# Second Mamba stage: C rows spread over partitions by DMA from DRAM, the leaky relu as a relu and one product more, sums in two banks, five chunks under way

## The reference, cut to what matters

```python
h = _mamba(_ln(src, n1_g, n1_b), ...)
src = src + _ln(h, mnorm_g, mnorm_b)
f = _ln(src, n2_g, n2_b) @ ffn_w1.T                     # 128 -> 512
f = jnp.where(f >= 0, f, 0.01 * f) @ ffn_w2.T           # leaky relu, 512 -> 128
src = src + f
src = src + (_ln(src, n3_g, n3_b) @ fe_w.T + fe_b)

# in _mamba, 16 states n for each of 128 features d:
x_c = silu(x_prev * conv_w[:, 0] + x_in * conv_w[:, 1] + conv_b)
dt, B, C = split(x_c @ x_proj_w.T, [64, 80])
delta = softplus(dt @ dt_proj_w.T + dt_proj_b)
h[d,n](t) = exp(delta[d] * A[n]) * h[d,n](t-1) + delta[d] * B[n] * x_c[d]
y[d] = sum over n of h[d,n] * C[n]
y = (y + x_c * Dp) * silu(z);  out = y @ out_proj_w.T
```

## Time and profile before

| | us |
|---|---|
| median of 3 runs | 3508.48 (3506.49 to 3509.16) |
| the profiled execution, its own time | 3504.51 |
| its span, first to last instruction | 3502.4 |
| first scan of MB | at 1870.30 |
| end of the last scan of MB | at 2315.7 |
| last weighting and add of M2's second pass | at 2539.16 |

### The profile page before, as it was taken

One profiled execution on the slowest core, in us unless ns is written; L12 is line 12 of the kernel. 1 busy time (PEld: TensorE's weight loads), 2 busy tenths in 40 slices (PEclk: granted clock), 3 DMA queues, 4 the chain that ended last, 5 costly groups with the idle time before them and its releaser, 6 DMA issues. The chain is left out here.

```text
span 3502.4 us, 45735 instructions
## 1 busy us (share of the span) xinstructions
PE 3090.4 (88%) x15266; PEld 1928.3 (55%) x15266; DVE 2466.9 (70%) x5491; ACT 2035.3 (58%) x3494; POOL 672.1 (19%) x547
## 2 busy tenths in 40 slices
PE   7998999998999996799887777778899998799998
PEld 5775334333777652256543333345477776577776
DVE  5557777773645877777666878776777777677776
ACT  4442767666445445444346766644387777277776
POOL 1020110100000000000003544430033333023332
PEclk9999999999999998889998999999999999799999
DMA  2000121110100320023330000013411110011011
GB/s 85 1 26 21 53 71 59 62 59 30 33 1 26 109 83 0 0 84 99 102 108 23 1 0 1 1 35 96 147 35 49 43 31 28 10 36 46 31 47 52
DMA packets 99186, 159.66 MB, mean 46 GB/s; under 512 B 16220, under 2 KB 28956, under 8 KB 98824
## 3 DMA queue, kind: packets, MB, share of 16 engines
q1 hardware_dynamic: 97368, 153.86, 14.1%
q10 hardware_dynamic: 1584, 2.88, 0.2%
HBM read 138.67 MB, written 17.99 MB: 45 GB/s over the span
## 5 line engine op out<-in xcount | busy, mean ns | idle before, releaser
L394 POOL TENSOR_TENSOR norm_rstd<-norm_rstd,minus_half 128x4 f32<-128x4 f32 x144 | 177.2, 1230 | 1530.6 <-DVE norm_rstd L385 1527.9
L2404 ACT ACTIVATE main_tiles_r<-banks,feature_cols 128x512 fp32r<-128x512 f32 x512 | 352.7, 689 | 186.5 <-PE banks L245 165.3
L2412 DVE TENSOR_TENSOR main_tiles_r<-main_tiles,main_tiles_r 128x512 fp32r<-128x512 f32 x512 | 382.9, 764 | 68.3 <-ACT main_tiles L2405 66.8
L243 PE MATMUL banks<-normed_pairs,moe_weights 128*128 128x512 f32 x800 | 407.8, 510 | 13.1 <-ACT main_tiles L2405 6.5
L955 DVE TENSOR_REDUCE gate_scratch<-banks 128x2 f32<-128x1024 f32 (+2 forms) x320 | 345.7, 1114 | 101.3 <-PE banks L234 51.5
L1113 ACT ACTIVATE main_tiles<-banks 128x512 f32<-128x512 f32 (+1 forms) x608 | 317.3, 578 | 154.9 <-PE banks L1099 56.4
L2405 ACT ACTIVATE main_tiles<-banks,feature_cols 128x512 f32<-128x512 f32 x512 | 349.9, 683 | 0.0
L2449 POOL TENSOR_TENSOR normed<-normed,main_tiles 128x512 f32<-128x512 f32 x128 | 217.7, 1700 | 532.0 <-DVE main_tiles L2438 532.0
L244 PE MATMUL banks<-normed_pairs,moe_weights 128*128 128x512 f32 x800 | 317.7, 397 | 0.0
L245 PE MATMUL banks<-normed_pairs,moe_weights 128*128 128x512 f32 x800 | 317.6, 397 | 0.0
L243 PE MATMUL banks<-main_tiles_r,moe_weights 128*128 128x512 f32 x640 | 267.4, 418 | 29.3 <-DVE main_tiles_r L2412 26.7
(11 more groups left out here) (355 smaller groups left out, 6851.9 us busy)
## 6 DMA issues: line engine op xcount, KB each, us to landing
main_tiles<-gates_d SPq DMA_DIRECT2D x400, 256.0 KB, 3.3
found_d<-main_tiles SPq DMA_DIRECT2D x32, 256.0 KB, 2.0
parts_d<-bf_parts SPq DMA_DIRECT2D x48, 128.0 KB, 1.8
q_stacks<-parts_d SPq DMA_DIRECT2D x192, 32.0 KB
k_stacks<-parts_d SPq DMA_DIRECT2D x192, 32.0 KB
weight_staging<-in_w SPq DMA_DIRECT2D x22, 256.0 KB, 3.8
attn_tiles<-in_w ACTq DMA_DIRECT2D x11, 256.0 KB, 7.6
x_res<-in_x_t SPq DMA_DIRECT2D x8, 256.0 KB, 9.2
```

The costliest lines, as they stand in the source:

```text
L243: eng.matmul(o, wh, hi, start=first, stop=False)
L394: eng.tensor_tensor(rstd[:, k, 1, :], rstd[:, k, 0, :], minus_half[:, :], ALU.pow).then_inc(s.norm_pow)
L2404: eng.activation(pair_3(j)[0], psum[:, 2 + j % 2, :], ACT.Relu, bias=bias)
L2412: eng.tensor_tensor(lo, h3_of(j), hi.bitcast(F32), ALU.subtract).then_inc(s.m3_lo)
```

## The change

- **C.** Products zc and copies cc go. ACT copies the C rows of the three-fold product bc (bank rows 64 to 96) into SBUF once per chunk ("cr"), SP writes 16 rows x 2 KB to DRAM (`c_rows_d`), and for each item SP issues a read of one row, broadcast to 128 partitions, into one of seven tiles. POOL waits for that DMA.
- **Leaky relu.** leaky(f) = relu(0.99 f) + 0.01 f. ACT writes relu(0.99 f); the 0.01 part becomes one product more in g, with a 128 x 128 matrix `folded` = 0.01 W2 W1, made once on PE and ACT when the stage begins. DVE L2225 goes.
- **Moved from DVE to ACT:** the conv's first product (L2184, now an ACT copy with scale, "cv") and the maximum in softplus (L2202, now ACT Relu, "m").
- **Sums** go to bank 2 or 4 by the chunk's parity; the first sum of a chunk waits for the chunk before the last.
- **Plan:** `LANES` 4 to 5, `MB_US` 59 to 46, item spacing 3.65 to 2.85, tail offsets pulled in (norm m 133.5 to 122.5, norm f 152 to 147, norm e 205 to 180, the final add 225 to 197; the front's stay), the second pass of M2 at `mb_at[7] + 134`. The lanes' semaphores are shared with the first Mamba's.

```diff
-    LANES = 4
-    MB_US, STATE_US, STATES_AT, PACE = 59.0, 3.65, 60.0, 1.3
+    LANES = 5
+    MB_US, STATE_US, STATES_AT, PACE = 46.0, 2.85, 60.0, 1.3
...
     def cc_of(q):
-        return wa_t[:, 23 + q % 4, :]
+        k = q % 7
+        return wa_t[:, 23 + k, :] if k < 5 else nat_t[:, k - 5, :]
+    def acc_of(i):
+        return psum[:, 4 if i % 2 else 2, :]
...
-            ("dt", 44.5, "dve", "m"), ("out", 125.6, "act", "oc"), ("f0", 170.0, "dve", "k0"), ("f1", 173.0, "dve", "k1"),
-            ("f2", 176.0, "dve", "k2"), ("f3", 179.0, "dve", "k3"), ("g", 187.0, "dve", "addf"), ("fe", 221.0, "dve", "fb"))
+            ("dt", 44.5, "act", "m"), ("out", 114.8, "act", "oc"), ("f0", 162.0, "act", "h0"), ("f1", 163.5, "act", "h1"),
+            ("f2", 165.0, "act", "h2"), ("f3", 166.5, "act", "h3"), ("g", 169.0, "dve", "addf"), ("fe", 193.5, "dve", "fb"))
...
                 elif name == "g":
-                    eng.wait_ge(*mb_dve(i, "k3"))
+                    eng.matmul(bank, folded, xn(("f", i)), start=True, stop=False)
                     for o in range(4):
...
+                        eng.wait_ge(*mb_act(i, f"h{o}"))
+                        z = eng.matmul(bank, w2n[:, w:w + P], hid_of(o), start=False, stop=o == 3)
...
+            eng.activation(xc_of(i), misc_bank(i, "x"), ACT.Copy, scale=col("m2conv", 1)).then_inc(sem)
...
+            eng.activation(c_rows, misc_bank(i, "bc")[64:96, :], ACT.Copy).then_inc(sem)
...
+            eng.activation(dl_of(i), misc_bank(i, "dt"), ACT.Relu, bias=col("m2dtb")).then_inc(sem)
...
-                eng.activation(hid_of(o), misc_bank(i, f"f{o}"), ACT.Copy, scale=0.01).then_inc(sem)
+                eng.activation(hid_of(o), misc_bank(i, f"f{o}"), ACT.Relu, scale=0.99).then_inc(sem)
...
-            eng.tensor_scalar(xc, v, col("m2conv", 1), None, ALU.mult).then_inc(s.mb_conv)
-            eng.tensor_scalar(dl_of(i), misc_bank(i, "dt"), col("m2dtb"), 0.0, ALU.add, ALU.max).then_inc(sem)
-                eng.tensor_tensor(hid_of(o), misc_bank(i, f"f{o}"), hid_of(o), ALU.max).then_inc(sem)
...
+    def sp_state_c(eng):
+        for q, i, n, when in state_items(-5.0):
+            if n == 0:
+                yield mb_at[i] + 46.5
+                eng.wait_ge(*mb_act(i, "cr"))
+                eng.dma_start(c_rows_d[i], c_rows[16:32, :]).then_inc(s.st_c_out, 16)
+            yield when
+            if n == 0:
+                eng.wait_ge(s.st_c_out, 16 * (i + 1))
+            if q >= 7:
+                eng.wait_ge(s.st_acc, q - 6)
+            eng.dma_start(cc_of(q), c_rows_d[i, n:n + 1, :].broadcast_to([P, C])).then_inc(st_c_in[q % 7], 16)
...
-            eng.wait_ge(s.st_cc, q + 1)
+            eng.wait_ge(st_c_in[q % 7], 16 * (q // 7 + 1))
...
-    plan_moe2(mb_at[-1] + 150.0)
+    plan_moe2(mb_at[-1] + 134.0)
```

More of the change, by code:

```diff
@@ L2086, in pe_mb @@
                     eng.wait_ge(*free())
-                elif misc_at[i, name][0] == 5:
-                    eng.wait_ge(s.m1_wt, 128)
                 else:
-                    eng.wait_ge(s.m1_done, 16)
+                    eng.wait_ge(s.fold_act, 1 if misc_at[i, name][0] == 5 else 2)
                 if name == "x":
@@ L2128, in act_mb @@
             eng.activation(tails[:, c, 0, 3:4], misc_bank(i, "x")[:, C - 1:C], ACT.Copy).then_inc(sem)
+            if i >= LANES:
+                eng.wait_ge(*mb_pe(i - LANES, "out"))
+            eng.activation(xc_of(i), misc_bank(i, "x"), ACT.Copy, scale=col("m2conv", 1)).then_inc(sem)
             yield t0 + 36.5
@@ L2180, in dve_mb @@
             v = misc_bank(i, "x")
-            eng.wait_ge(*mb_act(i, "tail"))
-            if i >= LANES:
-                eng.wait_ge(*mb_pe(i - LANES, "out"))
-            eng.tensor_scalar(xc, v, col("m2conv", 1), None, ALU.mult).then_inc(s.mb_conv)
-            eng.wait_ge(s.mb_conv, i + 1)
+            eng.wait_ge(*mb_act(i, "cv"))
             taken = eng.scalar_tensor_tensor(out=xc[:, 1:C], in0=v[:, 0:C - 1], scalar=col("m2conv", 0), in1=xc[:, 1:C],
@@ L2328, in pe_state_sum, with pe_fold, act_fold @@
             eng.wait_ge(s.st_y, q + 1)
-            eng.matmul(psum[:, 2, :], ident, cc_of(q), start=n == 0, stop=n == NS - 1).then_inc(s.st_acc)
-    on_pe += [*lanes(pe_mb, LANES), pe_state_zb, pe_state_zc, pe_state_sum]
-    on_act += [*lanes(act_mb, LANES), act_state_da, act_state_cc]
+            eng.matmul(acc_of(i), ident, cc_of(q), start=n == 0, stop=n == NS - 1).then_inc(s.st_acc)
+    def pe_fold(eng):
+        yield T_MB + 2.0
+        eng.wait_ge(s.m1_wt, 128)
+        eng.wait_ge(s.nat_in, 48)
+        for o in range(4):
+            w = N2["f1"] + o * P
+            z = eng.transpose(psum[:, 5, o * P:(o + 1) * P], w2n[:, w:w + P], ident)
+        z.then_inc(s.fold_pe)
+        yield T_MB + 6.0
+        eng.wait_ge(s.m1_done, 16)
+        eng.wait_ge(s.fold_act, 1)
+        for o in range(4):
+            w = N2["f2"] + o * P
+            z = eng.matmul(psum[:, 6, 0:P], hid_of(0)[:, o * P:(o + 1) * P], w2n[:, w:w + P], start=o == 0, stop=o == 3)
+        z.then_inc(s.fold_pe)
+    def act_fold(eng):
+        yield T_MB + 4.0
+        eng.wait_ge(*ma_dve(7, "x"))
+        eng.wait_ge(s.fold_pe, 1)
+        eng.activation(hid_of(0), psum[:, 5, :], ACT.Copy).then_inc(s.fold_act)
+        yield T_MB + 9.0
+        eng.wait_ge(s.fold_pe, 2)
+        eng.activation(folded, psum[:, 6, 0:P], ACT.Copy, scale=0.01).then_inc(s.fold_act)
+    on_pe += [pe_fold, *lanes(pe_mb, LANES), pe_state_zb, pe_state_sum]
+    on_act += [act_fold, *lanes(act_mb, LANES), act_state_da]
     on_dve += [*lanes(dve_mb, LANES), dve_state_db, dve_state_scan]
     on_pool += [pool_state_keep, pool_state_y]
-    plan_moe2(mb_at[-1] + 150.0)
+    on_sp.append(sp_state_c)
+    plan_moe2(mb_at[-1] + 134.0)
     M3_US, M3_CHUNK = 1.4, 47.0
```

106 lines of the change are left out of this document (50 added, 56 removed).

## The result

The changed kernel takes 3451.81 us (median of 4 runs, 3448.39 to 3456.91), the kernel before 3507.48 beside it (4 runs, 3505.64 to 3509.16). The ratio is 0.9843 [0.9826, 0.986], some 56 us less. The forecast was 70 us less (3438.5, range 3408 to 3476); the range holds the result, and the gain is four fifths of the forecast. The profiled execution took 3451.36 us, with a span of 3449.3.

A forecast was written before the change was run, and what follows sets the result against it. The states were taken as bound by DVE's work plus waits in a loop through in-order queues. Full chunks of 43.1 + 5.5 + 1.0 = 49.6 made the states 375.4 against 445.4, -70 in total: 3438.5 us, range 3408 to 3476.

The forecast's parts named there:

- DVE's work, 43.1 forecast: Full chunk: DVE loses conv product, maximum and four leaky maxima, 4.2 us, from 47.3 to 43.1.
- six table loads: ACT per chunk: an exponential falling between two Silus makes four loads where two did, +2.6 us; six in all.
- -1 behind the states: After the last scan: M2's routing uses bank 7 and cannot start before that scan, so only 1 us is gained.
- Of 5.0 I keep 1.0: DVE's waits for ACT's exponentials, per full chunk: mostly go without copies of C on ACT, 5.0 us to 1.0.
- The waits for B's spread stay: DVE's waits for PE's spread of B, per full chunk: stay because PE's list is bunched, 5.5 us in the sum.
- The 5 us of delay: PE from sum 0 to zb 7: 16.8 us of work in 11.6 of plan, so zb 7 comes 5 us late.
- Rival B: States: only work goes, no wait; full chunk 56.1 us, gain 26, time 3482; chance 0.14.
- Two banks, 0 forecast: Sums on PE: a chunk's first sum no longer waits for the chunk before; waits show nothing of weight, 0 us.
- A, the plan holds: States: full chunks run at the planned pitch of 46 us, gain 95, time 3413; chance 0.19.
- C fell: Rival C, C DMA: C arrives late, up to 5.3 us per chunk, pitch 55, time 3480; chance 0.05.
- D, the clock: PE: lower clock granted for most of the stage makes PE the bound; at 0.70, +46 us, 3555; chance 0.03.
- E fell: Rival E, ACT: a table switch costs double what the rows show, 22 us in all, time 3461; chance 0.01.

The follow-up runs named there:

- the version with two moves: Changed kernel with Silu of z planned at 36.7, not 37.4, norm steps 1.5 apart, not 1.3, and sums at 8.4, not 6.8: 3440.42 us, ratio 0.981.
- the norms at 1.5 alone: Changed kernel with Silu of z planned at 36.7, not 37.4, and norm steps 1.5 apart, not 1.3: 3446.94 us, ratio 0.9835.

## Why the prediction was right in kind and short in size

**The bound and the mechanism: right, and shown.** C through the in-order queues of PE and ACT held the exponentials. Putting it back (with the one sum bank that it needs, worth 2.2 of the 9.3 per chunk) undoes everything (0.9994), with DVE's work unchanged.

**DVE's work, 43.1 forecast, 44.6 measured.** The count was right, but two instructions are longer than they were (666 and 211 ns in the kernel before, on L2221 and L2190). Groups of DVE in the full chunks of the changed kernel (busy us, mean ns, idle), then the same in the version with two moves:

```profile
L2239 DVE TENSOR_TENSOR mamba_tiles<-mamba_tiles,normed 128x512 f32<-128x512 f32 x2 | 3.0, 1491 | 0.0
...
L2213 DVE SCALAR_TENSOR_TENSOR mamba_tiles<-conv_tails,feature_cols,mamba_tiles 128x1 f32<-128x1 f32 x3 | 2.6, 866 | 0.0
```

```profile
L2239 DVE TENSOR_TENSOR mamba_tiles<-mamba_tiles,normed 128x512 f32<-128x512 f32 x2 | 1.4, 676 | 0.0
...
L2213 DVE SCALAR_TENSOR_TENSOR mamba_tiles<-conv_tails,feature_cols,mamba_tiles 128x1 f32<-128x1 f32 x3 | 0.6, 204 | 0.0
```

With the same instructions on tiles of the other name, 0.8 and 0.7 per chunk are the 1.5. In the two-move version DVE is busy 173.2 / 4 = 43.3, the forecast's number. But this is no cause of the length: with the norms at 1.5 alone DVE is busy 43.4 and the chunk as long.

**PE 44.5 forecast, 44.3 measured; ACT 35.9 and 37.3; six table loads; SP, POOL and the C DMA at 0; -1 behind the states; second pass of M2 at 0**: right. Copies of ACT that follow one another overlap in the records, and taking 16 of them out removed less than their sum, which is my reading of ACT's 1.4 and was not tested. In the earlier trace rows a copy begins 0.09 before the record ahead of it ends (2123.95 + 0.72 against 2124.58); sixteen times that is 1.4, an estimate.

**The waits: the step that failed.** "Of 5.0 I keep 1.0" for the exponentials: 15.2 / 4 = 3.8 were measured. "The waits for B's spread stay", 5.5: 9.2 / 4 = 2.3. DVE in order of time shows the one long wait per chunk that was foreseen (idle before it in brackets), at less than half its size. The 5 us of delay were counted in the plan's clock with a period of 46 (its terms add up to 16.7 us of work, not 16.8); the period that ran is 52.4, which gives PE more room, a reading that was not tested:

```profile
2131.95 0.70 DVE L2289 TENSOR_TENSOR banks<-banks,mamba_tiles 128x512 f32<-128x512 f32 x1 [2.29 <-PE banks L2280]
```

Left out were 0.6 for the norms' statistics and 1.1 of small gaps. 44.6 + 3.8 + 2.3 + 0.6 + 1.1 = 52.4, where the forecast had 43.1 + 1.0 + 5.5 = 49.6. The small gaps could have been seen: of the 13.0 us without DVE's work before, the prediction named 11.7 and dropped 1.3. Where the 1.0 for the exponentials came from it does not say. The exponentials are late although ACT is idle 15 us per chunk, because its list holds it elsewhere, as here for a norm's product (ACT in order of time):

```profile
2112.59 0.78 ACT L457 ACTIVATE normed<-banks,feature_cols 128x512 f32<-128x512 f32 x1 [4.89 <-PE banks L439]
```

Whether those 5 us a chunk are the cause is not settled: spacing the norms wider took a third of them away (24.5 to 16.7 in four chunks), and the wait for exponentials stayed (14.7 and 15.5).

**The form of the sum failed with it.** Length = DVE's work + its waits is true of any trace, and as a forecast it supposes that a wait stays when another goes. Four maxima measured at 2.3 were worth 0.7; conv and maximum, 1.5 by their rows, were worth 0.4 in a full chunk; a wait for B of 2 per chunk came back as one for exponentials. Rival B, only work goes, had the sign of that error right (waits do not vanish) and its size wrong (56.1).

**Two banks, 0 forecast, 2.2 measured.** "The waits show nothing of weight there" was read in a plan where the loop of C came first; with that gone the bank shows. This term errs the other way: with a gain of 2.2 left out, the forecast was still 2.8 too short.

**The sum.** Chunks 2 to 6: 248 forecast, 261.5 measured. Chunk 0 41.4 and 40.7, chunk 1 45 and 46.3, chunk 7 41 and 43.8. Together 375.4 and 392.2. The 13.5 of the five full chunks are the bulk of the error of 17.

**Rivals.** A, the plan holds, fell: 46 was not reached by any version, and PE and DVE stand at 85% in full chunks. C fell: POOL never waited for the DMA. D, the clock: it fell from 0.94 to 0.91 in the full chunks and stayed over the 0.85 that was named as its sign; what that fall costs was not tested. E fell: a load begins, and its activation starts 1.30 later, as the rows of ACT show:

```profile
2130.43 1.28 ACT L2267 ACT_TABLE_LOAD   x1
2131.73 0.72 ACT L2267 ACTIVATE mamba_tiles<-mamba_tiles,neg_exp_alog 128x512 f32<-128x512 f32 x1
```

**What stays open.** Which chain sets 52.4, and why two moves together give 1.2 where each gives nothing, was not settled. The runs exclude table loads, DVE's stretched instructions and the block behind g as single causes; the norms' pace only as far as it was moved. The fifth lane and the earlier start of M2's second pass were never changed by themselves, so what either is worth is not shown.

## What to carry to other kernels

In in-order queues, first take out the round trip between engines, then tighten the plan: here the plan alone gave nothing and the operations alone about half. Do not price a freed wait or a freed instruction at its own length; ask which wait takes its place, and trust only the part that no other near-critical queue can give back. A buffer whose wait shows nothing before a change can be the next bound after it.

## What the runs showed of the hardware

DVE instructions with two inputs in SBUF can be held by POOL. DVE and POOL in order of time, changed kernel:

```profile
2128.79 0.87 DVE L2213 SCALAR_TENSOR_TENSOR mamba_tiles<-conv_tails,feature_cols,mamba_tiles 128x1 f32<-128x1 f32 x1
...
2142.45 1.46 DVE L2239 TENSOR_TENSOR main_tiles<-main_tiles,normed 128x512 f32<-128x512 f32 x1
```

```profile
2128.38 1.26 POOL L2327 TENSOR_TENSOR mamba_tiles<-mamba_tiles 128x512 f32<-128x512 f32 x1 [2.62 <-DVE mamba_tiles L2300]
...
2142.10 1.27 POOL L2327 TENSOR_TENSOR spare_nat<-spare_nat,mamba_tiles 128x512 f32<-128x512 f32 x1 [1.95 <-DVE mamba_tiles L2300]
```

Both begin while POOL's product runs. The first ends 0.02 us after it (2129.66 against 2129.64) and took 0.87; the second ends 0.54 after it (2143.91 against 2143.37) and took 1.46, as if its work had begun near POOL's end. Away from POOL's product the same two take 0.20 and 0.68. So even an instruction of a single column is held until POOL's product ends. The Trainium skill, SBUF — State Buffer, "Who interferes with whom", describes such a lock between a DVE operation with two SBUF inputs and a GpSimd one that reads SBUF: it is exclusive, and the order of issue decides which of the two blocks; these rows agree. They agree for the other order too. When DVE begins first, it keeps its 0.68 and POOL's product takes 1.70 instead of 1.27:

```profile
2098.39 0.68 DVE L2223 TENSOR_TENSOR mamba_tiles<-mamba_tiles 32x512 f32<-32x512 f32 x1
```

```profile
2098.50 1.70 POOL L2327 TENSOR_TENSOR mamba_tiles<-mamba_tiles 128x512 f32<-128x512 f32 x1 [0.69 <-DVE mamba_tiles L2300]
```

A product of PE can take twice its time. PE in order of time, changed kernel, two sums of the same form, and the two stretches they fill (length; busy PE, PEld, DVE, ACT, POOL; granted clock; DMA; GB/s):

```profile
2109.63 2.07 PE L2340 MATMUL banks<-mamba_tiles,const_mats 128*128 128x512 f32 x2 [1.31 <-POOL mamba_tiles L2327]
...
2116.88 1.02 PE L2340 MATMUL banks<-mamba_tiles,const_mats 128*128 128x512 f32 x2
```

```profile
2109.60:2111.70 2.10, 2.07 (x3) 0.93 (x4) 2.03 (x10) 0.00 (x0) 1.12 (x1) 0.51 0.00 0
2116.80:2117.95 1.15, 1.15 (x4) 0.48 (x3) 1.06 (x3) 0.60 (x1) 0.81 (x1) 1.00 0.01 2
```

The first took 2.07 at a granted clock of 0.51, the second 1.02 at 1.00: the two levels, 1.2 and 2.4 GHz. Before the first, PE had stood 2.20 us, done one spread in 0.39, and stood 1.31 more. Over whole chunks the clock does not follow PE's busy share: it was 0.91 in the changed kernel (busy 85%), 0.87 where sums waited for their one bank (83%), 0.88 with C through PE (80%), but 0.93 with the old plan (80%) and 0.94 in the kernel before (78%). Planning the sums so that PE does not wait for POOL took those waits away (8.5 us in four chunks to none), but PE then stood longer for the scans (17.7 to 34.2), and the clock stayed at 0.92. What lowers it was not found.
